# Row scatters of three batches issued back to back, and one more shared part run whole ahead of the expert blocks

## The chip, the core and the metric

One NeuronCore of one Trainium2 chip runs the whole kernel as one launch. The time is device microseconds (us) for one execution. The kernel before took 779.85 us as the median of three runs (778.77 to 779.91). Its engines are TensorE (PE, matrix products and transposes, with its weight loads as PEld), VectorE (DVE), ScalarE (ACT), GpSimd (POOL) and SyncE (SP). SP and POOL here do almost nothing but issue DMAs.

## The reference, cut to what matters

Inputs are 4 batches of 1024 tokens with 256 features, all in fp32.

```python
mod = (silu(c) @ wmod).reshape(4, 6, 1, 256)           # sa, ca, ga, sb, cb, gb
h = layernorm(x) * (1 + ca) + sa
x = x + ga * attention(h)                                # linear attention, 8 heads, conv of 5 taps, gate, Wo
h = layernorm(x) * (1 + cb) + sb
shared = silu(h @ Wsg.T) * (h @ Wsu.T) @ Wsd.T           # the shared expert, all 4096 tokens
p = softmax(h @ Wr.T)                                    # 32 experts
idx = top_k(p + bias, 6);  w = p[idx] / sum(p[idx])
y = sum over the 6 experts e of w_e * (silu(gate_e(h)) * up_e(h)) @ down_e.T
x = x + gb * (y + shared)
```

So each of 4096 tokens goes to 6 of 32 experts, and every token also goes through the shared expert.

## The kernel before

The work has three stages.

**Rounds.** A loop over b = 0 to 4 (`rounds`) does the attention of batch b (front) and, in the same round, the second norm, the router and the row making of batch a = b - 1 (back). For every token the router gives six slots, one in each chosen expert's region of the DRAM tensor `expert_rows`. A batch has 8 tiles of 128 tokens, so its rows are scattered by 8 x 6 = 48 indirect DMAs of POOL (`scatter_row`, L560), each for 128 rows of 1280 bytes. A batch may be scattered when its slots are known (`s_slot`, set by DVE at L1646) and its rows are copied (`wait_rows`). In the kernel before, POOL's 48 scatters of batches 0 and 1 (`scatter_through_round`) and of batch 2 (`scatter_through_middle`) are cut into groups of 2 to 4, and each group first waits for some step of PE in the round.

**Middle.** The shared expert is computed in 8 parts of 512 tokens. `ORDER` maps the part index i to a position in the token order. Parts 0 to `BEFORE` - 1 are run whole ahead of the blocks: `shared_gate(i)` and `shared_up(i)` (PE, L969, 4 matmuls of 128x512 each), a silu on ACT (L683), `shared_mid(i)` on DVE (L1524), `shared_down(i)` on PE (L998, 8 matmuls of 128x256) and `shared_add(i)` on DVE (L1531, L1532). Every matmul of fp32 appears as two in the trace. PE issues in the order that is written: the down of part 3, the up of part 4 and the down of part 4 stand last before the blocks. A down waits for its mid (`s_sm`) and for the add before it (`s_sx`). The columns of a part that is no longer in SBUF are read back from `h2_cols` by `load_h2(i)` on SP's queue.

**Blocks.** The scattered rows are taken in 224 blocks of 128 rows, two blocks to a duo, 112 duos (p). The table of blocks 0 to 111 needs only batches 0 to 2, so SP waits for their 144 scatters (`s_scat`, L482 and before), reads the table (L466) and loads 8 blocks to a group g (`load_blocks(g)`, L475). PE's order in duo p is `gate_up(p)` (L1330), `turn_blocks(p + 2)` (L1318) and `down(p - 2)` (L1345). ACT copies the expert weights (L898) and does the silu; DVE multiplies (L1839), keeps each block's weights and row numbers (`keep_meta`, L1852) and weighs the result (`weigh`, L1863) into a ring of 14 buffers, from which POOL scatters it to `expert_outs` (L664, "put"). Among its puts, POOL issues the scatters of the last batch: 16 of the 48 come ahead of the blocks, and then one after every third put, so that the last of them follows put 95. `load_blocks(14)`, for blocks 112 on, waits for all 48.

Parts in `AMONG` are not run ahead but in halves of 256 tokens, called units, among the blocks: a unit has its gate, up and down on PE in duos 1, 3 and 5 of a lap of 8 duos (`unit_gate` and `unit_up`, L1354; `unit_down`, L1379). `FIRST_UNIT` is 7 - the number of units, in laps. The columns of all parts in `AMONG` are loaded by SP at group g = `UNIT_LOADS` (= 2 `FIRST_UNIT`), after a wait for `s_table` to reach 3, which DVE sets at the end of lap 2 (L1832). The one part in `LAST` is run in the tail.

**Tail.** After the last block the six planes of each part are loaded and summed and the result is written out, part by part in the order `TAIL`.

The order of everything is written out by hand; there is no planner, and each engine has its own queue that is served in order.

## Time and profile before

| what | value |
|---|---|
| median of 3 runs | 779.85 us |
| profiled execution | 775.63 us, span 773.8 us |
| PE busy | 714.7 us (92%) |
| DVE, ACT, POOL busy | 482.6, 391.9, 410.9 us |
| chain that ended last, by engine | PE 65%, DVE 11%, POOL 11%, issue 5% |
| row scatters of POOL (L560) | 192, mean 1005 ns |
| puts of POOL (L664) | 224, mean 972 ns |
| 512 KB loads of shared columns (h_cols) | 5, median 4.1 us to landing |
| loads of blocks (expert_rows) | 224, median 2.9 us to landing |
| puts of POOL (expert_outs) | 224, median 3.4 us to landing |

The profile was taken of one execution, whose time is the 775.63 us above; its span starts at the first instruction. All positions below are us from that start. "Idle before" a row names what the engine waited for last. The chain is followed back from the last instruction, and a line on it is one that others waited for. The DVE rows of the tail, the PE rows of the rounds and of the blocks, and, between them, POOL's L560 stand on the chain.

### The profile page before, as it was taken

What the parts mean: (1) busy time and instruction counts of PE and PEld (TensorE: products, weight loads), DVE (VectorE), ACT (ScalarE), POOL (GpSimd) and SP (SyncE); (2) the same over time, 40 slices, a digit from 0 to 9 for tenths busy, and PEclk for the clock granted to TensorE, in tenths of its full rate; (3) what the DMA queues carried; (4) which work ended last, traced back from release to release, by engine and by line L of the source; (5) the groups of instructions that cost most, each with busy time, mean ns of one, the idle gap of its engine ahead of it and who ended that gap; (6) DMA issues with size and microseconds to landing.
All of it is one profiled execution on the core that took longest, in us unless ns stands there. A gap on an engine that the chain in (4) does not pass through costs nothing.

```text
span 773.8 us, 13345 instructions
## 1 busy us (share of the span) xinstructions
PE 714.7 (92%) x4326; PEld 586.9 (76%) x4326; DVE 482.6 (62%) x1258; ACT 391.9 (51%) x927; POOL 410.9 (53%) x420
## 2 busy tenths in 40 slices
PE   4988989998997998849999899999999999999994
PEld 3566668676676565549999899999999999998451
DVE  3887889799889628415555344444444545445998
ACT  5484755854661552126566455555565666654000
POOL 0000000667777777777777776774666666666100
PEclk9999999999999999969999999999999999999998
DMA  9510010243353998367777876775766666569995
GB/s 322 162 66 0 1 55 0 103 155 109 124 182 119 383 415 318 128 233 216 256 249 232 275 239 208 229 235 151 230 200 189 188 206 196 184 230 391 399 411 194
DMA packets 82620, 158.30 MB, mean 205 GB/s; under 512 B 14446, under 2 KB 55667, under 8 KB 82296
## 3 DMA queue, kind: packets, MB, share of 16 engines
q1 hardware_dynamic: 58344, 96.60, 37.9%
q0 software_dynamic: 19968, 56.67, 20.1%
q10 hardware_dynamic: 4240, 4.19, 1.6%
q8 instruction: 35, 0.57, 0.3%
q14 instruction: 33, 0.27, 0.1%
HBM read 88.02 MB, written 73.57 MB: 209 GB/s over the span
## 4 chain that ended last, share of the span: by engine, by line
PE 65%; DVE 11%; POOL 11%; issue 5%; ACT 4%; DMA 2%; SPq 1%; DVEq 0%; ACTq 0%; POOLq 0%
PE ps_wide L1330 17%; PE ps_wide L1345 12%; POOL expert_rows L560 11%; PE ps_kv L1330 8%; PE ps_narrow L1318 6%; PE ps_wide L1093 5%; PE ps_wide L1086 3%; DVE arena L1652 3%; PE ps_kv L1093 2%; PE ps_kv L1354 2%; PE ps_narrow L1045 1%; PE ps_kv L1423 1%; DVE arena L1912 1%; PE ps_narrow L1423 1%; DMA arena<-expert_rows 1%
## 5 line engine op out<-in xcount | busy, mean ns | idle before, releaser
L560 POOL DMA_INDIRECT expert_rows<-arena,slot_i x192 | 193.0, 1005 | 200.4 <-DVE arena L1646 136.8
L664 POOL DMA_INDIRECT expert_outs<-arena,meta x224 | 217.7, 972 | 108.3 <-DVE arena L1863 65.6
L898 ACT COPY arena<-arena 128x512 f32 x224 | 127.4, 616 | 153.3 <-PE ps_narrow L1318 146.1
L1863 DVE TENSOR_SCALAR arena<-ps_wide,meta 128x256 f32<-128x256 f32 x224 | 98.1, 480 | 127.2 <-PE ps_wide L1345 126.8
L1330 PEld LDWEIGHTS ps_wide<-arena 128*128 128x128 f32 x1200 | 146.5, 193 | 3.9 <-issue 0.2
L1330 PE MATMUL ps_wide<-arena 128*128 128x128 f32 x1200 | 147.2, 276 | 0.0
L1345 PE MATMUL ps_wide<-arena 128*128 x448 | 115.3, 380 | 0.9 <-DVE arena L1839 0.5
L1345 PEld LDWEIGHTS ps_wide<-arena 128*128 128x128 f32 x448 | 76.5, 190 | 7.3 <-issue 1.5
L1318 PE MATMUL ps_narrow<-cst,arena 128*128 128x128 f32 x448 | 68.8, 276 | 14.2 <-DMA arena<-expert_rows 14.2
L881 ACT COPY arena<-ps_narrow 128x512 f32<-128x512 f32 x112 | 64.7, 578 | 19.6 <-PE ps_narrow L1318 19.6
L1330 PEld LDWEIGHTS ps_kv<-arena 128*128 128x128 f32 x592 | 71.7, 192 | 1.9
L1330 PE MATMUL ps_kv<-arena 128*128 128x128 f32 x592 | 72.2, 275 | 0.0
L1318 PEld LDWEIGHTS ps_narrow<-cst,arena 128*128 128x128 f32 x448 | 53.0, 143 | 15.8 <-DMA arena<-expert_rows 14.0
L1839 DVE TENSOR_TENSOR arena<-arena,ps_wide 128x256 f32<-128x256 f32 x75 | 31.6, 421 | 38.2 <-ACT arena L889 38.1
L1093 PE MATMUL ps_wide<-arena 128*128 128x512 f32 x104 | 48.0, 605 | 0.5 <-ACT arena L767 0.5
L1852 DVE TENSOR_SCALAR meta<-arena 128x2 uint32 x224 | 31.2, 200 | 26.6 <-issue 25.4
L1652 DVE SCALAR_TENSOR_TENSOR arena<-arena 128x1024 f32<-128x1024 f32 x32 | 39.6, 1280 | 0.2
L969 PE MATMUL ps_wide<-arena 128*128 128x512 f32 x80 | 35.8, 596 | 0.0
L1093 PEld LDWEIGHTS ps_wide<-arena 128*128 128x128 f32 x104 | 19.9, 196 | 20.9 <-issue 19.8
L724 ACT ACTIVATE arena<-x,arena 128x256 f32<-128x256 f32 x56 | 28.3, 591 | 12.9 <-DVE arena L1467 12.9
L889 ACT ACTIVATE arena<-ps_wide 128x256 f32<-128x256 f32 x75 | 29.0, 386 | 2.3 <-PE ps_wide L1345 2.3
L1086 PE MATMUL ps_wide<-arena 128*128 128x256 f32 x128 | 29.1, 381 | 0.0
(241 smaller groups left out, 1017.8 us busy)
## 6 DMA issues: line engine op xcount, KB each, us to landing
arena<-expert_rows SPq DMA_DIRECT2D x224, 160.0 KB, 2.9
arena<-expert_outs SPq DMA_DIRECT2D x48, 512.0 KB, 12.4
arena<-w_experts SPq DMA_DIRECT2D x32, 384.0 KB, 15.8
expert_rows<-pad_row SPq DMA_DIRECT2D x33, 160.0 KB, 5.1
expert_outs<-arena,meta POOLq DMA_INDIRECT x224, 3.4
out<-x ACTq DMA_DIRECT2D x7, 512.0 KB, 11.6
x<-x SPq DMA_DIRECT2D x3, 1024.0 KB, 11.2
h_cols<-arena SPq DMA_DIRECT2D x6, 512.0 KB, 3.9
```

Of the source, the lines that this page charges most:

```text
L560: nc.gpsimd.indirect_dma_start(rows, bass.IndirectOffsetOnAxis(ap=slots_i[b % 2][:, t, k:k + 1], axis=0), hrows[b % 2][:, t, :], None, bou ...
L664: nc.gpsimd.indirect_dma_start(outs, bass.IndirectOffsetOnAxis(ap=meta_i[:, j % METAS, 1:2], axis=0), yb[j % OUTS], None, bounds_check=las ...
L881: nc.scalar.copy(xbt[:, p % 2, :], ps_narrow[:, p % 2]).then_inc(s_xbc, 1)
L898: last = nc.scalar.copy(wgu[:, j % 4:j % 4 + 1, :], wall[:, bass.ds(expert[j], 1), 0:DOWN])
L969: last = mm(ps_wide[:, slot, m], w[:, c, m * P:(m + 1) * P], shared_cols[i][c], start=(c == 0), stop=(c == C - 1))
L1086: last = mm(ps_wide[:, slot, i // 2, (i % 2) * D:(i % 2 + 1) * D], lhs[:, c, first:first + P], w[:, c, :], start=(c == 0), stop=(c == C - 1))
L1093: last = mm(banks[:, m], w[:, c, m * P:(m + 1) * P], rhs[:, c, hf * HALF:(hf + 1) * HALF], start=(c == 0), stop=(c == C - 1))
L1318: last = nc.tensor.transpose(ps_narrow[:, p % 2, (i * C + c) * P:(i * C + c + 1) * P], rows_in[:, u, c * P:(c + 1) * P], ident)
L1330: last = mm(bank[:, (half * DUO + i) * P:(half * DUO + i + 1) * P], wgu[:, (p * DUO + i) % 4, first:first + I], xbt[:, p % 2, (i * C + c) ...
L1345: last = mm(ps_wide[:, 1, p % 2, i * D:(i + 1) * D], hid[:, p % 2, i * P:(i + 1) * P], wall[:, bass.ds(expert[j], 1), DOWN:DOWN + D], star ...
L1652: last = v.scalar_tensor_tensor(lepe[:, c], vt[:, c, j:j + S], lw[:, c, j:j + 1], lepe[:, c], ALU.mult, ALU.add)
L1863: v.tensor_scalar(yb[j % OUTS], ps_wide[:, 1, p % 2, j % DUO * D:(j % DUO + 1) * D], meta[:, j % METAS, 0:1], None, ALU.mult).then_inc(s_y ...
```

## The change

Three things change. POOL loses all waits within the 48 scatters of batches 0, 1 and 2; what is left is the one wait per batch for its slots and rows. `BEFORE` goes from 5 to 6, so that part 5 is run whole ahead of the blocks, on all engines, and only part 7 is left in `AMONG` (two units instead of four). By the formulas above the first unit moves from lap 3 (duo 24) to lap 5 (duo 40) and its loads from group 6 to group 10. `LAST` is now part 6. SP gets one more load, of part 5's columns, behind the last experts' weights.

```diff
-BEFORE = 5
-LAST, AMONG = [BEFORE], [BEFORE + 1, BEFORE + 2]
-TAIL = [0, 1, 2, 3, LAST[0], 4] + AMONG
+BEFORE = 6
+LAST, AMONG = [BEFORE], [BEFORE + 1]
+TAIL = [0, 1, 2, 3, LAST[0], 4, 5] + AMONG
...
-                     + [tail_in[0], in_ranks, in_ranks, None])
+                     + [tail_in[0], h2t[:, :, 0:HALF], in_ranks, None])
...
-               + [tail_in[1], take(C, HALF, overlay=h2_at)])
+               + [tail_in[1], tail_in[0], take(C, HALF, overlay=h2_at)])
...
             for e in range(E - LATE, E):
                 sp.dma_start(wall[:, e], w_experts[:, e]).then_inc(s_wall, 16)
+            sp.wait_ge(s_su, 3)
+            load_h2(5)
...
-            def scatter_through_round(b):
-
-                r = b + 2
                 wait_rows(b)
-                scatter_rows(b, 0, 3)
-                pool.wait_ge(s_qkp, r * 4 + 1)
-                scatter_rows(b, 3, 5)
-                pool.wait_ge(s_qkp, r * 4 + 2)
...
-            for b in range(B - 2):
-                scatter_through_round(b)
-            scatter_through_middle(B - 2)
+            for b in range(B - 1):
+                wait_rows(b)
+                scatter_rows(b, 0, TILES * TOPK)
...
             shared_gate(4)
             shared_down(3)
             shared_up(4)
+            shared_gate(5)
             shared_down(4)
+            shared_up(5)
+            shared_down(5)
             turn_blocks(0)
...
             shared_mid(4)
             shared_add(4)
+            shared_mid(5)
+            shared_add(5)
             keep_meta(0)
```

On POOL, where the scatters of the first batch begin, stood (a row is a run of equal instructions, with what its first one waits for):

```order
L560 DMA expert_rows<-arena,slot_i 139392x320 [waits s_rows_copied,s_slots]
L560 DMA expert_rows<-arena,slot_i 139392x320 x2
L560 DMA expert_rows<-arena,slot_i 139392x320 [waits s_qk_projected]
L560 DMA expert_rows<-arena,slot_i 139392x320
L560 DMA expert_rows<-arena,slot_i 139392x320 [waits s_qk_projected]
L560 DMA expert_rows<-arena,slot_i 139392x320 x2
```

and now, for the first three batches:

```order
L563 DMA expert_rows<-arena,slot_i 139392x320 [waits s_rows_copied,s_slots]
L563 DMA expert_rows<-arena,slot_i 139392x320 x47
L563 DMA expert_rows<-arena,slot_i 139392x320 [waits s_rows_copied,s_slots]
L563 DMA expert_rows<-arena,slot_i 139392x320 x47
L563 DMA expert_rows<-arena,slot_i 139392x320 [waits s_rows_copied,s_slots]
L563 DMA expert_rows<-arena,slot_i 139392x320 x47
```

The scatters are the same and in the same order; the waits for PE's steps are gone.

On PE, between the ranks of the last batch and the first block, stood (L969 gate and up, L998 down, L1318 the turning of blocks):

```order
L1127 MATMUL ps_narrow<-seen,rcst 128x256
L969 MATMUL ps_wide<-arena 128x512 x8
L998 MATMUL ps_kv<-arena 128x256 x8
L969 MATMUL ps_wide<-arena 128x512 x8
L998 MATMUL ps_kv<-arena 128x256 x8
L969 MATMUL ps_wide<-arena 128x512 x4
L998 MATMUL ps_kv<-arena 128x256 x8
L1318 MATMUL ps_narrow<-cst,arena 128x128 x8
```

and now:

```order
L1057 MATMUL ps_narrow<-seen,rcst 128x256
L899 MATMUL ps_wide<-arena 128x512 x8
L928 MATMUL ps_kv<-arena 128x256 x8
L899 MATMUL ps_wide<-arena 128x512 x8
L928 MATMUL ps_kv<-arena 128x256 x8
L899 MATMUL ps_wide<-arena 128x512 x8
L928 MATMUL ps_kv<-arena 128x256 x8
L899 MATMUL ps_wide<-arena 128x512 x4
L928 MATMUL ps_kv<-arena 128x256 x8
L1248 MATMUL ps_narrow<-cst,arena 128x128 x8
```

Part 5's gate comes ahead of part 4's down, its up and its own down behind it: 16 matmuls more before the first block.

On PE in duo 25, where the first unit's gate was, stood (L1354 the unit's gate, L1330 gate_up of the next duo):

```order
L1330 MATMUL ps_wide<-arena 128x128 x8
L1318 MATMUL ps_narrow<-cst,arena 128x128 x4
L1345 ISA
L1345 MATMUL ps_wide<-arena 128x256
L1345 ISA
L1345 MATMUL ps_wide<-arena 128x256
L1354 MATMUL ps_kv<-arena 128x256 x4
L1330 MATMUL ps_kv<-arena 128x128 x8
```

and now:

```order
L1260 MATMUL ps_wide<-arena 128x128 x8
L1248 MATMUL ps_narrow<-cst,arena 128x128 x4
L1275 ISA
L1275 MATMUL ps_wide<-arena 128x256
L1275 ISA
L1275 MATMUL ps_wide<-arena 128x256
L1260 MATMUL ps_kv<-arena 128x128 x8
L1248 MATMUL ps_narrow<-cst,arena 128x128 x4
```

Six such groups of 4 matmuls (of 128x256) are gone from duos 25, 27, 29, 33, 35 and 37.

## Rows read from the trace of the kernel before

**Rows 1.** The waits of POOL: engine, line, awaited; total us, times, longest.

```profile
POOL expert_rows L560 <- issue: 56.4, 185, 0.3
POOL expert_rows L560 <- PE ps_wide L1101: 2.1, 1, 2.1
POOL expert_rows L560 <- PE ps_kv L1135: 2.1, 1, 2.1
POOL expert_rows L560 <- PE ps_wide L1086: 2.0, 2, 1.5
POOL expert_rows L560 <- PE ps_kv L1093: 0.7, 1, 0.7
```

**Rows 2.** Timeline, POOL: start, us, line, operation; scatters 1, 49 and 144.

```profile
137.22 1.13 POOL L560 DMA_INDIRECT expert_rows<-arena,slot_i  x1 [136.77 <-DVE arena L1646]
...
207.46 0.97 POOL L560 DMA_INDIRECT expert_rows<-arena,slot_i  x1 [0.30 <-issue]
...
331.16 0.97 POOL L560 DMA_INDIRECT expert_rows<-arena,slot_i  x1 [0.30 <-issue]
```

**Rows 3.** Timeline, DVE: the slots of batch 1.

```profile
198.38 0.17 DVE L1646 TENSOR_SCALAR arena<-arena 128x8 f32<-128x8 f32 x1
```

**Rows 4.** Timeline, PE, last shared steps and first blocks.

```profile
318.56 3.60 PE L969 MATMUL ps_wide<-arena 128*128 128x512 f32 x8
323.54 3.72 PE L998 MATMUL ps_kv<-arena 128*128 128x256 f32 x16 [1.38 <-DVE arena L1524]
337.86 0.69 PE L1318 MATMUL ps_narrow<-cst,arena 128*128 128x128 f32 x2 [10.60 <-DMA arena<-expert_rows]
...
341.80 2.84 PE L1330 MATMUL ps_wide<-arena 128*128 128x128 f32 x16
...
344.92 1.95 PE L1330 MATMUL ps_wide<-arena 128*128 128x128 f32 x16
```

**Rows 5.** The chain of waits, the load of block 0: start, us, what.

```profile
335.36 0.36 SPq L475
```

**Rows 6.** Windows: stretch, length, busy of PE, PEld, DVE, ACT, POOL, granted clock, DMA.

```profile
327.30:341.80 14.50, 2.26 (x8) 1.46 (x9) 2.76 (x4) 1.62 (x3) 11.12 (x12) 0.59 0.56 184
```

**Rows 7.** Timeline, PE, gate_up of duos 26 and 27.

```profile
424.97 1.95 PE L1330 MATMUL ps_kv<-arena 128*128 128x128 f32 x16
...
431.02 1.95 PE L1330 MATMUL ps_wide<-arena 128*128 128x128 f32 x16
```

**Rows 8.** The chain of waits, 419 to 430 and one step of a unit.

```profile
419.19 0.33 SPq L425
...
425.18 4.07 DMA arena<-expert_rows
...
434.27 1.73 PE ps_kv L1354 x8
```

**Rows 9.** Timeline, POOL: puts 0 and 39, and the last row scatter.

```profile
352.87 0.97 POOL L664 DMA_INDIRECT expert_outs<-arena,meta  x1 [0.30 <-issue]
...
419.44 0.97 POOL L664 DMA_INDIRECT expert_outs<-arena,meta  x1 [0.30 <-issue]
...
520.70 0.98 POOL L560 DMA_INDIRECT expert_rows<-arena,slot_i  x1 [0.30 <-issue]
```

**Rows 10.** Timeline, SP: loads of blocks 112 and 113.

```profile
524.30 0.89 SPq L475 DMA_DIRECT2D arena<-expert_rows  x2
```

**Rows 11.** Timeline, PE: the turning of duos 56 and 57.

```profile
535.14 0.60 PE L1318 MATMUL ps_narrow<-cst,arena 128*128 128x128 f32 x4
...
538.23 0.60 PE L1318 MATMUL ps_narrow<-cst,arena 128*128 128x128 f32 x4
```

**Rows 12.** Timeline, POOL and DVE, in the round of batch 2.

```profile
168.29 1.57 POOL L560 DMA_INDIRECT expert_rows<-arena,slot_i  x1 [2.13 <-PE ps_wide L1101]
170.16 1.81 POOL L560 DMA_INDIRECT expert_rows<-arena,slot_i  x1 [0.30 <-issue]
...
169.85 2.47 DVE L1652 SCALAR_TENSOR_TENSOR arena<-arena 128x1024 f32<-128x1024 f32 x2
```

More of the change, by code:

```diff
@@ L614, in scatter_through_middle @@
-            def scatter_through_middle(b):
-                wait_rows(b)
-                scatter_rows(b, 0, 3)
-                pool.wait_ge(s_sg, 1)
-                scatter_rows(b, 3, 6)
-                pool.wait_ge(s_su, 1)
-                scatter_rows(b, 6, 9)
-                pool.wait_ge(s_sg, 2)
-                scatter_rows(b, 9, 12)
-                pool.wait_ge(s_sd, 1)
-                scatter_rows(b, 12, 15)
-                pool.wait_ge(s_tr2, (B - 1) * PAIRS + 2)
-                scatter_rows(b, 15, 18)
-                pool.wait_ge(s_tr2, (B - 1) * PAIRS + 4)
-                scatter_rows(b, 18, 20)
-                pool.wait_ge(s_su, 2)
-                scatter_rows(b, 20, 24)
-                pool.wait_ge(s_sg, 3)
-                scatter_rows(b, 24, 28)
-                pool.wait_ge(s_rowt, (B - 1) * PAIRS + 2)
-                scatter_rows(b, 28, 31)
-                pool.wait_ge(s_rowt, (B - 1) * PAIRS + 4)
-                scatter_rows(b, 31, 34)
-                pool.wait_ge(s_sd, 2)
-                scatter_rows(b, 34, 38)
-                pool.wait_ge(s_rank, B)
-                scatter_rows(b, 38, 42)
-                pool.wait_ge(s_su, 3)
-                scatter_rows(b, 42, TILES * TOPK)
```

33 lines of the change are left out of this document (removed).

## The prediction

> **What bounds the kernel now.** I read the chain of waits by line first. It is PE almost everywhere, with one stretch in which POOL's row scatters carry it. So there are three places to look at, and each was read in the timeline of its engines.
>
> The first is POOL before the blocks. Its first scatter starts at 137.22, its 144th at 331.16 [rows 2]. All between is POOL at its own rate: a scatter every 1.28 us (0.97 busy, 0.30 to issue), 143 x 1.278 = 182.8 us, where 193.9 passed. The rest is 11.1 us. The list of POOL's waits says what part of it is waiting for PE: 2.1 + 2.1 + 2.0 + 0.7 = 6.9 us in five waits [rows 1], and since each holds the usual 0.30, the loss is 5.4 us. All the other paced waits found their step of PE long done. The remaining 5.6 us are scatters that ran long (1.57 and 1.81 us, [rows 12]).
>
> The second is the way into the blocks. PE ends the down of part 4, which starts at 323.54, at 327.0 (16 x 0.2155), and then has nothing for 10.6 us, until block 0 has landed at 337.86 [rows 4]. The chain shows what it waits for: scatter 144 [rows 2], its landing and SP's read of the table, and the load at 335.36 [rows 5], 4.2 us after the scatter's start. [...]
>
> The third is the blocks. A duo takes 3.09 us of PE without a pause (535.14 to 538.23, [rows 11]). Whatever else PE does there is added: a unit's gate is 1.73 us on the chain [rows 8], and its up and down are as many matmuls of that shape. One more pause stands at the turning of duo 28: gate_up(26) starts at 424.97, gate_up(27) behind that turning at 431.02 [rows 7], 6.05 where a duo takes 3.09, so 2.96 us lost. The chain leads back to SP, which sat at its wait for the finished second table until 419.19 [rows 8] and could then first load columns of parts 6 and 7 and write padding; the blocks for duo 28 were asked for at 424.6 and took 4.07 us [rows 8].
>
> **The change, part by part.** The sum is made against the profiled execution, 775.63 us; the median of the runs is 4.2 us above it, and I carry the difference over to the median.
>
> *Waits of POOL.* The 5.4 us go. What could be late next is the rows themselves: batch 1 is ready at 198.55 [rows 3], and POOL now comes to it at 207.46 - 5.4 = 202.1 [rows 2], still 3.5 us behind it; batch 2 is ready with more in hand, since the rounds and 48 scatters both take some 61 us. So scatter 144 starts at 325.8 and SP asks for block 0 at 330.0. The fourth block was turned directly ahead of gate_up(0), at 341.80 - 0.88 = 340.9, 5.6 us after the first load [rows 4, 5]; so all four are there by 335.6.
>
> *Part 5 ahead of the blocks.* PE's new work is gate, up and down, 3 x 3.45 us. Step by step: gate(5) 321.99 (318.56 + 3.43, [rows 4]), in the 1.4 us pause in which PE waited for the mid of part 4 and beyond it; down(4) 325.4, up(5) 328.9; down(5) waits for the mid of part 5 as down(4) did for its own, 4.98 us after the start of the up (318.56 to 323.54), so 333.85; end 337.3. Turning duo 0 takes 0.87, ACT's copy of it 0.6 and the way there and back 0.3, so gate_up(0) starts at 339.15. PE wants the first row at 337.3 and they were there at 335.6, so PE is now last, by 1.7 us. Before it was 341.80: 2.65 us gained. With a pause of only 1.4 us ahead of it PE keeps its clock, and gate_up(1) follows after 4 x 0.11 + 16 x 0.11 = 2.22 instead of 3.12 us: 0.9 more. **3.55 us** in all. If the clock fell all the same, at least this 0.9 would be lost again. ACT's silu and DVE's mid and add of part 5 run beside PE; behind them on ACT and DVE stand the weight copies and the keeping of blocks 0 to 3, which are not wanted before PE has turned them, and both engines were busy for 1.6 and 2.8 of 14.5 us there [rows 6]. SP's new load is issued when the up of part 2 is done (about 301.5) behind the last five experts; with the 4.1 us of such a load in the table above, or three times that, it is there before 322. Behind it on SP stands only the first table, which is needed at 328.
>
> *Two units fewer among the blocks.* 6 groups of 1.73 us on PE's path [rows 8]: **10.38 us**. The cover for this is that PE sets the duo and not another engine, which the pace of 3.09 in duos without a unit shows. What is added elsewhere for it has been counted above.
>
> *SP's wait for the second table.* It moves from group 6 to group 10, far behind the table. SP then keeps up as it did in groups 3 to 5, and the pause of **2.96 us** goes. The two remaining loads at group 10 cost SP some 0.9 us; the blocks are loaded 9 us ahead of their use and take 2.9, so it is hidden.
>
> *What is late next: POOL among the blocks.* POOL is served in order, and for every three blocks it has three puts and a scatter: 352.87 to 419.44 is 52 of them, 1.280 us each [rows 9], so 3.41 us a duo where PE takes 3.09. Before, units and the pause at duo 28 gave POOL the time to catch up. Now it falls behind until duo 40. From put 0 at 347.5 (352.87 - 5.4) 127 steps of 1.280 lead to the last row scatter at 510.1, and the lag, at most some 12 us, stays under the 18 at which the ring of 14 buffers would stop DVE (14 x 1.54 less the 3.4 us that a put takes to land). But `load_blocks(14)` waits for that scatter: 3.6 us from its start to the load (520.70 to 524.30, [rows 9, 10]) makes 513.7, 0.5 for the second block and 3.7 to 4.1 to land [rows 7, 8] makes 517.9 to 518.3. PE wants them at 535.14 - 3.55 - 2.96 - 10.38 = 518.25 [rows 11]. So this wait takes over almost exactly. If POOL's scatters lose 1 us in the rounds to contention (next paragraph) it is 1.1 us late. I charge **0.7 us**, between 0 and 4.
>
> *What scatters cost where they now fall.* Next to the DVE instruction of 2.47 us at 169.85 (two of 128x1024 with all operands in SBUF) the scatter took 1.81 us [rows 12]; the one at 168.29 had been held back by a wait for 2.1 us, while four such DVE instructions ran. Unpaced, one or two scatters fall on these. The price is between nothing (most scatters beside DVE work are 0.97) and 0.84 each for some two; it is off the path before the blocks by the 1.7 us, and in the 0.7 above.
>
> [...]
>
> **The sum.** 3.55 + 10.38 + 2.96 - 0.7 = 16.2 us. 775.63 - 16.2 = 759.4 for a profiled execution, 779.85 - 16.2 = **763.7 us** for the median.
>
> **Rivals.**
> 1. *POOL's backlog becomes the bound.* If its mean step among the blocks is 1.31 instead of 1.28, the last row scatter is 3.8 us later and PE waits that much more at duo 56: 767.5. For it: POOL has no slack left in 40 duos. Against: the 52 steps of before ran at 1.280. Chance 0.16.
> 2. *The back to back scatters gain nothing*, since what they no longer wait for they lose to DVE. Then block 0 is where it was, PE waits 4 us for it, the clock may fall, only some 0.5 to 0.9 of the 3.55 us remain, and duo 56 is 4 to 5 us late: 16.9 - 2.8 - 4.5 = 9.6, so 770.2. Chance 0.07.
> 3. *Slower than before.* The same mechanism at full size: unpaced scatters run beside the rounds' DVE work all the time. Before the blocks there are 1.7 us of slack, then each microsecond is paid; with 16.2 us of gain it turns into a loss beyond some 18 us, that is 0.126 us for each of 144 scatters, a mean step of 1.44. At 1.5 it is 779.85 + (0.18 x 144 - 18) = 788. For it: single scatters of 1.57 and 1.81. Against: 185 of 192 scatters already had nothing but the issue ahead of them [rows 1]. Chance 0.03.
> 4. *The changed kernel is better than the sum*: POOL is not late at duo 56 and a pause or two that I did not count goes as well: 761.5 to 762.5. Chance 0.14.
> 5. *It does not do what it says*: most removed waits did nothing. That is so, and is in the sum, as only 5.4 us of them are counted.
>
> The forecast itself has 0.60, within 762.5 to 765.5. The range of 8 in 10 is 761.3 to 769: it takes in rivals 1 and 4 and part of 2. A difference under 0.2% (1.6 us) could not be told from none: faster 0.96, same 0.01, slower 0.03.
>
> **What would show it.** Five waits of POOL for PE are gone and scatter 144 starts near 326. PE's pause before block 0 falls from 10.6 us to under 2, and the granted clock there stays at 1.00. gate_up(0) starts at 339 and gate_up(27) stands 3.1 us behind gate_up(26). No L1284 group (the units' new line) comes before duo 41. POOL waits for nothing up to duo 40 or so, and PE has a pause of 0 to 2 us at the turning of duo 56, behind a block's DMA. The tail is as long as before. The forecast is wrong if POOL's step grows, if the clock falls at 330 in spite of all, or if the duos of 24 to 40 take more than 3.09 us.

## The result, and the profile after

The changed kernel takes 760.14 us (median of 4 runs, 759.39 to 760.64), the kernel before beside it 779.88 us (778.77 to 780.91). The ratio is 0.975, with a 95% interval of 0.9735 to 0.9764: 19.7 us less, where 16.2 were forecast. The time lies 1.2 us under the low end of the range.

The profiled execution of the changed kernel took 759.68 us (span 757.7), where the sum had 759.4 for it. So the sum is almost exact against the profiled execution of before and 3.5 us short against the median. Its steps come first.

The waits of POOL in the changed kernel (L563 is the row scatter, L594 the put; columns as in [rows 1]):

```profile
POOL expert_rows L563 <- DVE arena L1579: 137.0, 1, 137.0
POOL expert_rows L563 <- issue: 57.6, 189, 0.3
POOL expert_outs L594 <- DVE arena L1796: 52.4, 80, 1.7
POOL expert_outs L594 <- issue: 44.4, 144, 0.8
POOL expert_rows L563 <- PE ps_wide L1260: 0.9, 1, 0.9
POOL expert_rows L563 <- PE ps_kv L928: 0.5, 1, 0.5
```

Against [rows 1], 6.9 us of waits for PE in the rounds are gone. The two that are left hold 0.9 and 0.5 us and belong to scatters of the last batch.

The timeline of POOL: scatter 144, put 0 and the last row scatter, which answer to [rows 2, 9]:

```profile
325.34 0.97 POOL L563 DMA_INDIRECT expert_rows<-arena,slot_i  x1 [0.30 <-issue]
...
347.93 0.97 POOL L594 DMA_INDIRECT expert_outs<-arena,meta  x1 [0.30 <-DVE arena L1796]
...
511.05 0.98 POOL L563 DMA_INDIRECT expert_rows<-arena,slot_i  x1 [0.30 <-issue]
```

Scatter 144 is 5.8 us sooner than in [rows 2] (forecast 5.4).

The timeline of PE on the way into the blocks, which answers to [rows 4] (L899 gate and up of the shared parts, L928 their down, L1248 turning, L1260 gate_up):

```profile
329.40 3.60 PE L899 MATMUL ps_wide<-arena 128*128 128x512 f32 x8
334.38 3.72 PE L928 MATMUL ps_kv<-arena 128*128 128x256 f32 x16 [1.38 <-DVE arena L1457]
337.94 1.04 PE L1248 MATMUL ps_narrow<-cst,arena 128*128 128x128 f32 x8
339.22 2.05 PE L1260 MATMUL ps_wide<-arena 128*128 128x128 f32 x16 [0.24 <-ACT arena L811]
...
341.54 1.95 PE L1260 MATMUL ps_wide<-arena 128*128 128x128 f32 x16
...
343.76 1.95 PE L1260 MATMUL ps_kv<-arena 128*128 128x128 f32 x16
```

The 10.60 us in which PE waited for block 0 [rows 4] are gone: the turning follows the down of part 5 with no idle time ahead of it. The windows of the same stretch as [rows 6] show the work that took their place and the clock:

```profile
327.30:341.80 14.50, 12.88 (x66) 9.65 (x65) 6.74 (x9) 3.04 (x6) 10.30 (x12) 1.00 0.65 216
```

PE is busy for 12.88 us where it was for 2.26, and was granted its full clock (1.00) where it had 0.59.

PE in duos 26 and 27, which answer to [rows 7]:

```profile
419.53 1.95 PE L1260 MATMUL ps_kv<-arena 128*128 128x128 f32 x16
...
422.62 1.95 PE L1260 MATMUL ps_wide<-arena 128*128 128x128 f32 x16
```

3.09 us apart, where [rows 7] has 6.05. SP loads blocks there and no longer waits for the second table.

Duo 56 on PE, and SP's load of block 112, which answer to [rows 10, 11]:

```profile
516.32 1.95 PE L1260 MATMUL ps_wide<-arena 128*128 128x128 f32 x16
518.19 0.86 PE L1248 MATMUL ps_narrow<-cst,arena 128*128 128x128 f32 x4
519.39 1.12 PE L1275 MATMUL ps_wide<-arena 128*128 x4 [0.34 <-issue]
520.35 0.83 PE L1260 MATMUL ps_wide<-arena 128*128 128x128 f32 x6
```

```profile
514.52 0.89 SPq L478 DMA_DIRECT2D arena<-expert_rows  x2
```

From gate_up(54) at 516.32 to gate_up(55) it is 4.03 us instead of 3.09. This is the new wait. It doesn't show as one pause of PE: the turning takes 0.86 us where 0.60 is usual, and 0.34 us of idle time follow. Its size varies: when the changed kernel ran again (below), the same stretch took 4.84 us, 1.75 more than 3.09.

The chain of the page by engine, of the changed kernel:

```profile
PE 74%; DVE 18%; ACT 6%; issue 2%; DMA 1%; DVEq 0%
```

POOL had 11% of the chain before and is off it now.

| step | forecast | profiled execution after |
|---|---|---|
| scatter 144 | 325.8 | 325.34 |
| gate_up(0) | 339.15 | 339.22 |
| gained by gate_up(2) | 3.55 | 3.38 (347.14 - 343.76) |
| gained from there to gate_up(28) | 6.42 (two units' groups 3.46, pause 2.96) | 6.75 |
| gained by gate_up(54) | 16.9 | 17.03 (533.35 - 516.32) |
| last row scatter | 510.1 | 511.05 |
| lost at duo 56 | 0.7 | 0.94 (4.03 - 3.09) |
| gained by gate_up(111) | 16.2 | 16.09 (708.86 - 692.77) |
| time of the profiled execution | 759.4 | 759.68 |
| **median of the runs** | **763.7** | **760.14** |

gate_up(0) agrees through two misses that cancel: the down of part 5 starts at 334.38 where the sum had 333.85, because PE was already 0.5 us later at the up of part 4 (319.08 for 318.56), and the turning with its copy took 0.4 us less than forecast.

### The profile page after: what moved, and what is told of

The parts are those of the page before. It is cut to its first block, busy times and chain, and to the rows that moved or that the text cites. A ratio compares the mean times of both kernels' runs of the same rounds, so it can differ in the third digit from the quotient of the medians.

```text
span 757.7 us, 13311 instructions
## 1 busy us (share of the span) xinstructions
PE 712.7 (94%) x4310; PEld 583.8 (77%) x4310; DVE 482.9 (64%) x1255; ACT 391.6 (52%) x926; POOL 410.6 (54%) x420
## 4 chain that ended last, share of the span: by engine, by line
PE 74%; DVE 18%; ACT 6%; issue 2%; DMA 1%; DVEq 0%
PE ps_wide L1260 18%; PE ps_wide L1275 13%; PE ps_kv L1260 9%; PE ps_narrow L1248 6%; PE ps_wide L1023 5%; PE ps_wide L899 5%; DVE arena L1585 4%; PE ps_wide L1016 3%; PE ps_kv L928 2%; PE ps_kv L1023 2%; PE ps_narrow L975 2%; PE ps_kv L1356 1%; DVE arena L1847 1%; PE ps_narrow L1356 1%; ACT arena L635 1%
## 5 line engine op out<-in xcount | busy, mean ns | idle before, releaser
L563 POOL DMA_INDIRECT expert_rows<-arena,slot_i x192 | 192.4, 1002 | 196.1 <-DVE arena L1579 137.0
L594 POOL DMA_INDIRECT expert_outs<-arena,meta x224 | 218.1, 973 | 96.8 <-DVE arena L1796 52.4
L1260 PEld LDWEIGHTS ps_wide<-arena 128*128 128x128 f32 x1200 | 145.5, 192 | 4.4 <-ACT arena L811 0.5
L1260 PE MATMUL ps_wide<-arena 128*128 128x128 f32 x1200 | 146.4, 275 | 0.2 <-ACT arena L811 0.2
L1275 PEld LDWEIGHTS ps_wide<-arena 128*128 128x128 f32 x448 | 76.5, 190 | 7.3 <-issue 1.5
L1260 PEld LDWEIGHTS ps_kv<-arena 128*128 128x128 f32 x592 | 71.8, 192 | 1.9
L1260 PE MATMUL ps_kv<-arena 128*128 128x128 f32 x592 | 72.2, 275 | 0.0
L1248 PE MATMUL ps_narrow<-cst,arena 128*128 128x128 f32 x448 | 67.3, 273 | 0.0
L1248 PEld LDWEIGHTS ps_narrow<-cst,arena 128*128 128x128 f32 x448 | 52.7, 142 | 0.4 <-DMA arena<-expert_rows 0.2
L1023 PE MATMUL ps_wide<-arena 128*128 128x512 f32 x104 | 47.1, 596 | 0.5 <-ACT arena L697 0.5
L899 PE MATMUL ps_wide<-arena 128*128 128x512 f32 x96 | 42.8, 595 | 0.0
L1785 DVE TENSOR_SCALAR meta<-arena 128x2 uint32 x224 | 31.6, 202 | 16.9 <-issue 16.9
L1023 PEld LDWEIGHTS ps_wide<-arena 128*128 128x128 f32 x104 | 19.6, 193 | 20.3 <-issue 19.3
L899 PEld LDWEIGHTS ps_wide<-arena 128*128 128x128 f32 x96 | 18.0, 190 | 20.0 <-issue 19.8
L613 ACT ACTIVATE arena<-ps_wide 128x1024 f32<-128x1024 f32 x7 | 7.1, 1021 | 47.9 <-PE ps_wide L899 47.9
```

Of the source, the lines that this page charges most:

```text
L563: nc.gpsimd.indirect_dma_start(rows, bass.IndirectOffsetOnAxis(ap=slots_i[b % 2][:, t, k:k + 1], axis=0), hrows[b % 2][:, t, :], None, bou ...
L594: nc.gpsimd.indirect_dma_start(outs, bass.IndirectOffsetOnAxis(ap=meta_i[:, j % METAS, 1:2], axis=0), yb[j % OUTS], None, bounds_check=las ...
L899: last = mm(ps_wide[:, slot, m], w[:, c, m * P:(m + 1) * P], shared_cols[i][c], start=(c == 0), stop=(c == C - 1))
L1023: last = mm(banks[:, m], w[:, c, m * P:(m + 1) * P], rhs[:, c, hf * HALF:(hf + 1) * HALF], start=(c == 0), stop=(c == C - 1))
L1248: last = nc.tensor.transpose(ps_narrow[:, p % 2, (i * C + c) * P:(i * C + c + 1) * P], rows_in[:, u, c * P:(c + 1) * P], ident)
L1260: last = mm(bank[:, (half * DUO + i) * P:(half * DUO + i + 1) * P], wgu[:, (p * DUO + i) % 4, first:first + I], xbt[:, p % 2, (i * C + c) ...
```

## The experiments

Seventeen runs follow. The kernel before ran beside them on every chip, and the chips fall into two kinds: on three of them before takes 779.0 to 779.5 us, about as in the result above (first kind), on two others 854.6 and 860.3 us (second kind). Which chip a kernel runs on couldn't be chosen, and each of the five chips was used for one group of runs at one time only. So "kind of chip" is a name for what was met: whether it belongs to the chip, or to something else that held on it at that time, isn't shown. The two kinds are told apart below, since they answer different questions.

### Does one profiled execution stand for the kernel before?

**The kernel before again** (no edit), first on a chip of the second kind and then of the first.

> The kernel before, unchanged, once more. The span of the changed kernel is 16.1 us shorter than that of the one profiled execution before (757.7 against 773.8), but the medians are 19.7 apart, because that one execution (775.63) was 4.2 us under its own median (779.9). Theory A: the way into the blocks varies, since PE stands idle there for 10.6 us and comes back at half clock; then this run's profile, if its time is near 779.9, has its first gate_ups later than 341.8 by some 4 us or a longer half-clock stretch, and all else as before. Rival B: the pause at duo 28 varies (SP and its loads): then gate_up(27) is later by 4 us more. Rival C: the rounds vary (the first scatter starts 4 us later than 137.2), which would be nothing of the change. If it comes out at 775.6 again the question stays.

> The kernel before, for a profile of an ordinary execution. Where before takes 780 its executions spread from 776.0 to 782.0 with mean granted clocks from 0.980 down to 0.970, and those of the changed kernel only from 760.0 to 760.9. Theory A: PE idles 10.6 us ahead of the blocks and is then at half clock for a time that differs from one execution to the next; an execution near 780 has the half-clock stretch near 330 longer than the 13.65 us of the first profile, by some 7 us, and gate_up(2) about 3.5 us later than 347.1. Rival B: the pause at duo 28 is longer. Rival C: the other dips, in the rounds, are longer.

Measured: 861.22 us on the second kind, ratio to its own twin beside it 1.0005 (0.9967 to 1.0042); 780.07 us (778.94 to 780.67, 10 runs) on the first, 1.0006 (0.9992 to 1.002). On the first kind the profiled execution took 779.09 us (span 777.3), 0.8 under the median in the result, and is called the ordinary one below. This is the timeline of its PE at the turning of duo 28, beside [rows 7]:

```profile
426.29 1.95 PE L1330 MATMUL ps_kv<-arena 128*128 128x128 f32 x16
431.12 1.32 PE L1318 MATMUL ps_narrow<-cst,arena 128*128 128x128 f32 x4 [2.88 <-DMA arena<-expert_rows]
432.51 2.07 PE L1345 MATMUL ps_wide<-arena 128*128 x4
434.38 2.07 PE L1330 MATMUL ps_wide<-arena 128*128 128x128 f32 x16
```

gate_up(26) to gate_up(27) takes 8.09 us here, and 6.05 in [rows 7]. The wait for the block is 2.88 us, and behind it the work itself is slow: 1.32 for a turning of 4 (0.60 elsewhere), 2.07 for a down of 4 (1.03). The windows show the clock:

```profile
327.30:342.90 15.60, 3.01 (x12) 1.74 (x11) 2.95 (x4) 1.62 (x3) 11.94 (x13) 0.66 0.56 178
426.90:438.00 11.10, 8.15 (x47) 6.68 (x46) 1.75 (x6) 3.09 (x7) 8.51 (x9) 0.85 0.95 312
```

The granted clock is 0.85 over the second stretch: 0.50 for 3.4 us from 431.2 on, behind the pause, and 1.00 from 434.6 to 438. In the profiled execution that the forecast rested on, PE waited for the same blocks in two pieces, and the clock stayed at 1.00 (PE's timeline and the window of that stretch):

```profile
428.37 0.44 PE L1318 MATMUL ps_narrow<-cst,arena 128*128 128x128 f32 x2 [1.45 <-DMA arena<-expert_rows]
429.29 0.44 PE L1318 MATMUL ps_narrow<-cst,arena 128*128 128x128 f32 x2 [0.48 <-DMA arena<-expert_rows]
```

```profile
424.50:434.00 9.50, 7.24 (x51) 6.32 (x51) 1.79 (x8) 2.98 (x6) 7.31 (x8) 1.00 1.02 365
```

Here is the difference to that execution:

| position | before, first profile | before, ordinary | difference |
|---|---|---|---|
| up of part 4 | 318.56 | 319.43 | 0.9 |
| scatter 144 | 331.16 | 332.02 | 0.9 |
| gate_up(0) | 341.80 | 342.97 | 1.2 |
| gate_up(2) | 347.14 | 348.80 | 1.7 |
| gate_up(24) | 416.63 | 418.29 | 1.7 |
| gate_up(28) | 435.83 | 439.31 | 3.5 |
| gate_up(111) | 708.86 | 712.33 | 3.5 |
| span | 773.8 | 777.3 | 3.5 |

So the 3.5 us lie in three places: 0.9 is there before PE comes to the up of part 4, that is in the rounds, 0.8 is lost from there to gate_up(2), and 1.8 at the pause ahead of duo 28. Nothing is lost after it. The second and the third are what the change takes away; the first it leaves alone. Of the theories above, A is refuted as it was put: the stretch at half clock (granted 0.50) is 13.7 us long in both executions, from 330.0 on in the first profile and from 332.2 in the ordinary one, and gate_up(2) is 1.7 us later and not 3.5. B has the largest share (1.8), C has 0.9, and 0.8 are left for the way into the blocks. This is one pair of executions; no other execution of before on this kind of chip has a trace.

**The changed kernel again**, on a third chip of the first kind.

> The changed kernel once more, as the standard for the three kernels beside it. Where the kernel before takes some 780 us: 759.4 to 760.7, ratio 0.975. Where it takes some 855 to 860: 955 to 965, ratio 1.12.

Measured: 759.63 us (758.8 to 760.29), ratio 0.9748 (0.9713 to 0.9784), as in the result. The kernel before beside it ran in 775.47 (mean granted clock 0.980), 776.50 (0.978), 778.06 (0.978), 779.01 (0.975), 779.90 (0.976), 780.46 (0.974) and 780.86 us (0.974), a spread of 5.4 us that goes with the clock. On the chip of the next section it doesn't: there before ran in 776.92 and in 781.38 us at 0.975 and 0.974. So what sets the time of a single execution is only in part the clock. The four executions of the changed kernel spread over 1.5 us, at 0.986 or 0.987. Over all chips of the first kind the kernel before lies between 775.47 and 782.03 in the 32 runs beside the experiments; one of them was faster than the profiled 775.63 us.

### The change in parts, on chips of the first kind

**The scatters back to back alone.** Of the change only this:

```diff
-            for b in range(B - 2):
-                scatter_through_round(b)
-            scatter_through_middle(B - 2)
+            for b in range(B - 1):
+                wait_rows(b)
+                scatter_rows(b, 0, TILES * TOPK)
```

> Only the waits in POOL's scatters removed. If before takes 780 here: rows 5.8 us earlier, PE's pause some 5 us. Theory A adds that the stretch at half clock is shorter and less varied: 5.8 us by the rows and up to 3.5 of clock: 771 to 774, with a spread of executions of 2 us or less. Rival: 779.9. If before takes 860 here: 960.

Measured: 773.97 us (772.58 to 774.71), ratio 0.9935 (0.9912 to 0.9957): 5.1 us faster. PE on the way into the blocks (L925, L1245, L1257 are the down, the turning and gate_up):

```profile
324.63 3.72 PE L925 MATMUL ps_kv<-arena 128*128 128x256 f32 x16 [1.38 <-DVE arena L1451]
332.62 1.50 PE L1245 MATMUL ps_narrow<-cst,arena 128*128 128x128 f32 x4 [4.26 <-DMA arena<-expert_rows]
...
336.68 2.55 PE L1257 MATMUL ps_wide<-arena 128*128 128x128 f32 x11
```

Without part 5 PE still waits for block 0, but 4.26 us and not 10.60. gate_up(2) starts at 342.38, 6.4 us sooner than in the ordinary execution of before. The pause ahead of duo 28 is still there, and dearer: the clock is at half for 6.8 us there (0.50 from 424.6 to 431.5), and gate_up(24) to gate_up(28) takes 22.4 us for 21.0. With that 1.4 us are given back up to gate_up(111).

**Part 5 ahead of the blocks alone**, with the paced scatters kept.

```diff
-BEFORE = 5
+BEFORE = 6
...
+            shared_gate(5)
             shared_down(4)
+            shared_up(5)
+            shared_down(5)
...
```

> Only part 5 ahead, scatters paced. If before takes 780 here: rows at 341, PE's pause 4 us, units 10.4 and the pause at duo 28 3.0 gained, duo 56 waits 3 to 5 us for the last scatters: 766 to 770. Rival (the halves add up): 766.6 and no more wait at duo 56 than 0.95. If before takes 860: 868.

Measured: 764.33 us (761.11 to 767.37), ratio 0.9809 (0.9762 to 0.9857), under the 766 to 770 expected. It is 4.2 us above the changed kernel's median on another chip. At duo 56 its PE (L1321 turning, L1348 down, L1333 gate_up) stands thus:

```profile
517.27 1.95 PE L1333 MATMUL ps_wide<-arena 128*128 128x128 f32 x16
519.50 0.44 PE L1321 MATMUL ps_narrow<-cst,arena 128*128 128x128 f32 x2 [0.28 <-DMA arena<-expert_rows]
521.12 0.44 PE L1321 MATMUL ps_narrow<-cst,arena 128*128 128x128 f32 x2 [1.19 <-DMA arena<-expert_rows]
522.08 2.07 PE L1348 MATMUL ps_wide<-arena 128*128 x4 [0.52 <-issue]
523.94 2.69 PE L1333 MATMUL ps_wide<-arena 128*128 128x128 f32 x16
```

Two duos take 6.67 and 3.83 us, so 4.3 are lost where the changed kernel loses 0.94: POOL's row scatters are later (the last at 513.3), and again the clock falls behind the pause (0.50 for 3.4 us from 522.1 on). So the two parts of the change aren't independent, and the rival is wrong: POOL's earlier start also pays at duo 56.

**The units and their loads one lap later alone**, which is meant to take only the pause ahead of duo 28 away; nothing of PE's work is moved out of the blocks.

```diff
-FIRST_UNIT = FULL // UNROLL - len(UNITS)
+FIRST_UNIT = FULL // UNROLL - len(UNITS) + 1
...
-                if g == HALFWAY + 1:
+                if g == HALFWAY + 4:
```

> The kernel before with its four units one lap later. If before takes 780 here: 3.0 to 3.3 us less, 776.7, if the pause at duo 28 was SP's wait for the second table; rival: 779.9, the pause only moved. If before takes 860: no difference to be told (863 against 860 in the run before).

Measured: 774.27 us (773.91 to 774.93), ratio 0.9938 (0.9914 to 0.9961): 4.8 us. PE at gate_up(26) to (28):

```profile
424.62 1.95 PE L1329 MATMUL ps_kv<-arena 128*128 128x128 f32 x16
...
427.70 1.95 PE L1329 MATMUL ps_wide<-arena 128*128 128x128 f32 x16
...
430.79 1.95 PE L1329 MATMUL ps_wide<-arena 128*128 128x128 f32 x16
```

The pause is gone, and it hasn't moved elsewhere: from gate_up(28) to gate_up(54) it takes 95.8 us, which is 26 duos at 3.09 and nine groups of a unit at 1.73 (95.9). So it was SP's wait, and not the start of a unit. It was worth 4.8 us in the medians and 5.1 in the traces (712.33 - 707.27 at gate_up(111), beside the ordinary execution), where 3.0 to 3.3 were expected and the sum has 2.96. By the three traces that have the pause it costs 3.3 us (first profile), 5.1 (ordinary) and 6.5 (scatters back to back alone), each from gate_up(24) to (28), less this kernel's 12.45 and two groups of a unit. This shows that the pause is dearer in the ordinary execution than in the one first profiled, and that it varies. That it makes the spread of the runs isn't shown: this kernel spans 1.0 us over six runs and before beside it 4.8 over 17, but the second copy of before on the same chip, with the pause, spans 1.7 over ten.

### The pauses left at duo 56

The changed kernel with two more of the last batch's scatters ahead of put 0, and the same with the paced scatters of before kept:

```diff
-AHEAD = 16
+AHEAD = 18
```

> The changed kernel with AHEAD = 18 instead of 16, so that the last row scatter of the last batch follows put 89 instead of put 95: six steps of POOL, 7.7 us, sooner. The scatter at 511.05 comes at about 503.4, block 112 lands some 7 us ahead of its use and the pause of 0.95 us at the turning of duo 56 goes. If my reading of that pause is right, 0.9 us faster than the changed kernel beside it on a chip where before takes 780: 759.2. Rival: the two more scatters ahead of put 0 make put 0 later by 2.6 us, the lag of POOL reaches the ring of 14 buffers near duo 40, and DVE is held back: no gain, 760 to 762. On a chip where before takes 860 it stays with the changed kernel at 1.12.

> Before with part 5 ahead of the blocks, its paced scatters kept, and AHEAD = 18. Where before takes 780: the wait of 4.3 us at duo 56 that part 5 alone has goes, so 4 us faster than that (764.3): 760.3, as the changed kernel. Rival: put 0 comes 2.6 us later and the ring holds DVE back: 763 to 765. Where before takes 860: as part 5 alone, 1.00 to 1.01, and far from the changed kernel's 1.12; it would then be the version to take on both.

Measured, beside the changed kernel's 759.63 on the same chip: 758.86 us (758.49 to 758.94) and 762.51 us (761.88 to 763.57). The last row scatter of the first (POOL) and PE's duo 54:

```profile
502.47 0.98 POOL L563 DMA_INDIRECT expert_rows<-arena,slot_i  x1 [0.31 <-issue]
```

```profile
516.08 1.95 PE L1260 MATMUL ps_wide<-arena 128*128 128x128 f32 x16
517.86 0.60 PE L1248 MATMUL ps_narrow<-cst,arena 128*128 128x128 f32 x4
518.30 1.03 PE L1275 MATMUL ps_wide<-arena 128*128 x4
519.17 1.50 PE L1260 MATMUL ps_wide<-arena 128*128 128x128 f32 x12
```

With the scatter 8.2 us sooner (510.7 in the changed kernel beside it) the duo takes 3.09 again, where it took 4.84 in that one. So the wait at duo 56 was POOL's backlog, as the sum had it, and the ring of 14 buffers holds out against the two added steps. This version is the fastest of all, if only by 0.8 us in the median (1.8 in the traces, but there the changed kernel's is the slowest of its four runs); one of the changed kernel's four runs (758.80) is as fast. The second was expected at 760.3 and takes 762.51: its wait at duo 56 is gone too (3.09), so the rival of the ring is wrong, but it comes into the blocks later than part 5 alone did in its profile (gate_up(2) at 346.92 for 344.72). Of these 2.2 us, 1.3 are there at POOL's first scatter already (136.91 for 135.63), so they are of the rounds.

The two kernels of this pair differ only in the pacing of the scatters: 3.65 us in the median, and 3.39 us in the traces at gate_up(2) (346.92 and 343.53). That is the price of the pacing in this pair, once nothing waits at duo 56.

### What happens on chips of the second kind

**The same three parts and the change itself.**

> Only the waits within POOL's scatters are removed; part 5 stays in units. My accounting: the rows are there 5.8 us earlier, PE's pause before block 0 falls from 10.6 to some 5 us, gate_up(0) 336.0, the pause at duo 28 and all units stay: about 5.8 to 6.7 us less than before (773.5 by the median). Rival: POOL's work was not what the blocks waited for, or the unpaced scatters cost the rounds as much: no change (779.9).

> Only part 5 is run ahead, POOL's scatters stay paced. My accounting: rows at 341, so PE pauses some 4 us before the blocks and gate_up(0) stays near 341.5; units 10.4 and the pause at duo 28 3.0 are gained, and POOL, 5 us later into the blocks, makes PE wait 3 to 5 us at duo 56: 9 to 11 us less than before by profile (769 to 771 by the median). Rival: the two halves of the change are independent and add up: 13.3 us less (766.6), with no more pause at duo 56 than the 0.95 us of the changed kernel.

> The kernel before with its four units one lap (8 duos) later, in laps 4 to 7, so that SP's wait for the second table comes at group 8 instead of 6; the load of the last part's columns comes three groups later. Nothing else is changed. If the pause at duo 28 was SP's wait, it goes: 3.0 to 3.3 us less than before (776.7 by the median). Rival: the pause was the cost of starting units (loads of columns and the DMA they take): then it comes back in duo 34 to 36 and the time is as before (779.9).

> The kernel with only the waits within POOL's scatters removed, again. If before takes 780 here: 773.5 by my accounting (rows for the blocks 5.8 us earlier, all of it on the path, the clock a little sooner up). If before takes 860 here: 960 as in the run before, with DVE's wait for the second half of K of up to 43 us in each of the rounds 2 and 3.

> The changed kernel once more, beside the kernel before on the same chip. In the runs so far the kernel before took 780 us at first and 860 us in the later runs, where engines waited for semaphores that had long been raised, while POOL issued. Theory A: what makes a kernel slow there is POOL issuing scatters without a pause; then, on a chip where before takes 860, the changed kernel takes 940 to 970 like the kernel with the waits removed alone (963); on one where before takes 780, it takes 760. Rival: part 5 ahead of the blocks makes up for it: 860 or less beside 860.

| kernel | us | ratio to before beside it |
|---|---|---|
| scatters back to back alone | 962.88 | 1.1194 (1.1114 to 1.1275) |
| the same, other chip | 951.47 | 1.117 (1.1065 to 1.1276) |
| part 5 alone | 868.39 | 1.0108 (1.0065 to 1.015) |
| units a lap later alone | 863.09 | 1.0035 (0.9993 to 1.0077) |
| the whole change, other chip | 960.73 | 1.1246 (1.115 to 1.1343) |

The same program that gains 2.5% on one chip loses 12% on another, and the unpaced scatters alone account for it. The other two parts, which gain on the first kind, gain nothing here (1.011 and 1.004); why is left open. The 12% are lost ahead of the blocks: gate_up(0) starts at 478.42 with them and at 371.11 in before on the same chip, and from there to gate_up(111) it is 416.7 and 419.6 us. The windows from 137 to 200, where POOL issues its first 48 scatters, of before and of the unpaced kernel, both on the second kind:

```profile
137.00:200.00 63.00, 59.05 (x301) 43.83 (x300) 55.36 (x134) 38.76 (x105) 44.29 (x42) 0.97 0.35 124
```

```profile
137.00:200.00 63.00, 27.48 (x89) 15.57 (x87) 17.41 (x31) 17.49 (x59) 47.45 (x48) 0.75 0.35 124
```

PE, DVE and ACT do a half to a third of their work while POOL keeps its rate (a scatter every 1.29 us), and the DMA share is the same 0.35 in both. So a slow POOL is not the cause, and no more data is moved in the one than in the other. The waits of the unpaced kernel show what stands still, and the timelines of PE, DVE and ACT one instance:

```profile
ACT arena L727 <- remote: 140.0, 8, 45.3
ACT arena L825 <- remote: 135.4, 37, 7.6
...
DVE arena L1469 <- remote: 79.2, 2, 43.6
```

```profile
153.79 2.54 PE L1013 MATMUL ps_wide<-arena 128*128 128x256 f32 x11
...
198.34 0.97 POOL L560 DMA_INDIRECT expert_rows<-arena,slot_i  x1 [0.30 <-issue]
...
202.43 2.35 DVE L1469 TENSOR_TENSOR arena<-ps_wide,arena 128x1024 f32<-128x1024 f32 x2 [43.57 <-remote]
...
205.24 1.93 ACT L727 ACTIVATE arena<-ps_narrow,arena 128x256 f32<-128x256 f32 x4 [37.09 <-remote]
```

"remote" is an awaited semaphore whose rise fits the end of no instruction near it. PE's K projection (L1013) ends at 156.33; DVE's L1469, which waits for it, starts at 202.43. In the trace's record of the semaphore itself, the increment of that matmul stands at 202.40, 46 us late and 4 us after the start of the last of the 48 scatters. ACT's wait is alike: increments of matmuls at 161 and 168 us are recorded at 205.2. On the first kind the very same kernel has the increment of that matmul at 156.86, 0.02 us after its end at 156.84. So the increments of other engines arrive late while POOL issues one indirect DMA after the other, in this state of the chip. In before, 42 scatters fall into the same window with waits between them, and that stretch is not touched (59.05 us of PE there against 59.10 on the first kind). What before loses on these chips comes later: 29 us up to gate_up(0) and 53 in the blocks, where POOL issues puts (in its list of waits, ACT's L898 waits 119.2 us for "remote" in 34 times). That the puts are the cause there is read from the waits and not tested. The waits for "remote" sum up to 342 to 490 us in each of the six traces of the second kind, and there is none in any trace of the first, with or without pacing.

**Is it the waits, or POOL's standing still?** The changed kernel with groups of 3 scatters between waits that were long satisfied, with such a wait before every scatter, and with groups of 16 between which POOL waits until they have landed.

```diff
-                scatter_rows(b, 0, TILES * TOPK)
+                for n in range(0, TILES * TOPK, 3):
+                    if n:
+                        pool.wait_ge(s_slot, 1)
+                    scatter_rows(b, n, n + 3)
```

> The changed kernel, with a wait before every third scatter of batches 0 to 2 on a semaphore that was raised long ago (s_slot at 1), so that POOL has as many waits as before but none that holds it. Theory A (where before takes 860 us, the other engines' semaphore increments are delivered late while POOL issues without any wait between, and a wait alone lets them through): 860 or less instead of 960. Rival B (what helps there is that POOL is held back until the others have come on, so that its stream has real pauses): about 960, as without waits. Where before takes 780: both say 760, since a raised wait costs nothing.

> The same with such a raised wait before every scatter. Theory A: 860 or less, and less than with every third. Rival B: about 960. Where before takes 780: 760.

> The changed kernel, with two waits in each batch of scatters, after 16 and after 32, for the batch's own scatters to have landed: a pause of some 2 us in which POOL's queue runs empty. Theory B (only a real pause lets the increments through): an engine can be held for 20 us at most instead of 45, so 860 to 900 where before takes 860. Theory A: nearly as slow as without (940 to 960), since two waits in 48 scatters are few. Where before takes 780: 8 to 12 us over 760, since 6 pauses of 2 us fall on POOL's path and 1.7 us of it are hidden.

> The changed kernel with POOL's 48 scatters of batches 0 to 2 cut into groups of 3, and a wait between the groups on a semaphore that has long been raised. Where before takes 780 it costs 0 to 0.8 us against the changed kernel. Where before takes 860, two theories: if any wait instruction between scatters is enough for the other engines' semaphore increments to get through, the ratio is about 1.01, as with only the part moved; if what helped in the kernel before was that POOL really stood still at some of them, it stays at 1.12.

All four ran on chips of the first kind: 760.30 us (ratio 0.9767, 0.9731 to 0.9802), 760.90 (0.9771, 0.9735 to 0.9807), 772.07 (0.9908, 0.9874 to 0.9942) and 759.63 (0.9749, 0.9713 to 0.9785), the last equal to the changed kernel's 759.63 on the same chip. So satisfied waits cost under a microsecond against the 760.14 above, and drains of the queue 12, all as expected for this kind. Of the question they were made for they say nothing: it stays open which property of the pacing lets the increments through on the second kind.

## Why the prediction was wrong

*The sum was right* for the execution that it was made against. Its terms are found in the trace of the changed kernel within 0.4 us: 3.38 for 3.55 at the start of the blocks, 6.75 for 6.42 up to duo 28, 0.94 for 0.7 at duo 56, 16.09 for 16.2 in all. Part of the closeness is luck: two misses of 0.5 and 0.4 us cancel at gate_up(0), the last row scatter is 0.95 us later than forecast (511.05 for 510.1), and duo 56 cost 1.75 us in another execution. The clock stayed up (1.00 from 327.3 to 341.8), POOL's step stayed at 1.28, and its lag came to some 13 us at most where some 12 were said. Of the 3.55, 0.9 are the 3.12 us from gate_up(0) to gate_up(1) [rows 4], for which PE was granted 0.70 of its clock, less an estimated 2.22: in the changed kernel the two stand 2.32 us apart (339.22 to 341.54), at 1.00. The pause of 1.38 us ahead of the last down left the clock at 1.00 in both kernels.

*The step that failed* is the last one: "the median of the runs is 4.2 us above it, and I carry the difference over to the median". It treats the 4.2 us as something that lies around the kernel and that the changed kernel would have as well. The changed kernel's profiled execution is only 0.5 us under its median. Most of the difference lay inside the kernel before, in the very pauses that were costed. Its profiled execution was among the fastest it has (one of the 32 runs beside the experiments is faster). Term by term, with the changed kernel's profile set against each of the two traces of before:

| term | forecast | against the first profile | against the ordinary execution |
|---|---|---|---|
| rounds, up to the up of part 4 | 0 | -0.52 | 0.35 |
| from there to gate_up(2) | 3.55 | 3.90 | 4.69 |
| pause ahead of duo 28 | 2.96 | 3.29 | 5.11 |
| six groups of a unit | 10.38 | 10.36 | 10.36 |
| duo 56 | -0.7 | -0.94 | -0.94 |
| sum, at gate_up(111) | 16.2 | 16.09 | 19.57 |

So the mechanism was right, and two terms were sized too small for an ordinary execution: the pause ahead of duo 28 (2.96, measured 5.11) and the way into the blocks (3.55, measured 4.69). The 19.6 of the last column and the 19.7 between the medians agree so well by some luck, since both executions lie under their medians, by 0.8 and 0.5 us.

*What is in it.* The pause is the part that is shown, by taking it alone away: 4.8 us in the medians and 5.1 in the traces. The sum priced it at what PE lost in an execution in which the clock stayed at 1.00 behind it; in the ordinary one 3.4 us at half the clock (0.50) follow. The way into the blocks is read from two traces and not isolated: beyond what the sum had, 0.3 lies between scatter 144 and gate_up(0), 0.5 is a longer way to gate_up(1) (3.61 us at a granted 0.60, for 3.12 at 0.70), and the rest is the shorter turning. What comes from the rounds is chance and nothing of the change: up to 140 us the first profile of before has 3.4 us at half clock, the ordinary one 6.8, and the changed kernel 6.8 in both of its traces of this kind. Of this 0.9 us between the two executions of before, the changed kernel's own profile has 0.5.

The pause of 2.88 us in the ordinary execution is followed by work at half the clock (0.50 from 431.2 to 434.6), and the changed kernel, without the pause, has 1.00 there (415 to 430). The first profile of before, where the wait came in two pieces of 1.45 and 0.48 us, had 1.00 as well, but with part 5 alone the clock fell behind waits of 0.28 and 1.19 us (0.50 for 3.4 us from 522.1 on). What sets the clock in general isn't shown.

*The rivals.* Rival 1 (POOL's backlog sets the bound) was right in its place and wrong in size and reason: POOL's step stayed at 1.28, and the wait is 0.94 to 1.75 us, with the paced scatters 4.3. Rival 2 is refuted: scatter 144 moved by 5.8 us, as many as the removed waits held and more. Of the 144 scatters before the blocks six run over 1.2 us, where nine did before, so back to back they are held up no more often. Rival 3, slower than before, was given 0.03, and it depends on the chip: on the kind where the kernel was measured it is false, on the other it is true by 12%. That the time was not of the second kind was luck as far as the prediction goes. Its mechanism was another: the scatters themselves keep their step while the other engines' increments are held up. No row of the profile of before spoke of this. Rival 4 named the right side, a better result than the sum, but 761.5 to 762.5 was still too high, since I looked for uncounted pauses and not for the counted ones being larger.

*The range.* It ended at 761.3, 2.4 us under the forecast. The runs shown spanned 1.1 us and the profiled one lay 3.1 us under the lowest of them: that was in view. Asking where those 4.2 us were would have given a second forecast of 759.5 (all of it in the pauses) to 763.7 (none of it), and a range that starts near 759.

## What to carry to other kernels

When the profiled execution is clearly faster or slower than the median of the runs, take a second profile before its durations are used, and look first at the pauses behind which TensorE's clock falls (to 0.50 here). Here they made three quarters of the difference; if the change removes such a pause, count its share as gained too. Two changes that look independent can share a later cover: here the earlier scatters paid a second time at duo 56, and a constant that shifts a backlog by six steps was worth another 0.8 us. And a long run of back to back indirect DMAs on GpSimd may be free on one chip and cost 12% on another (ratios of 0.9935 and 1.1194 here), so a kernel that will run on several is to be timed on several.

## What the runs showed of the hardware

The same program takes 779 to 780 us on some chips and 855 to 860 on others, and what the traces show to differ is how late semaphore increments arrive while GpSimd issues indirect DMAs (up to 46 us here, at a scatter every 1.29 us). GpSimd keeps that pace through the 48 scatters, while other engines stand idle with their inputs ready (VectorE for 43.57 us at L1469, ScalarE for 37.09 at L727). Each chip was met once, so that this is a lasting property of a chip isn't shown.

A pause of TensorE cost more here than it waited. The one ahead of duo 28 is 2.88 us of waiting in the ordinary execution and costs 5.0 us (8.09 - 3.09), with 3.4 us at half the clock (0.50) behind it.
